# Sigmoid attention, last batch: unit 2 sorted earlier with a second set of rows, unit 3's root behind the last sigmoid

## The chip, the core and the metric

The kernel runs on one core of a Trainium2 chip. A core has five engines that run side by side and wait for each other by semaphores: TensorE (PE, matrix products), VectorE (DVE), ScalarE (ACT), GpSimd (POOL) and SyncE (SP, which only issues transfers). The metric is the device time of one execution in microseconds (us), lower is better.

## The reference

A block of four layers on x of 4 x 1024 tokens with 128 features: a sigmoid attention, an expert layer (8 experts, the best 2 of each token), a softmax attention, and the expert layer again. Only the end of the first and the start of the second matter here:

```python
q = jnp.einsum('bsd,ed->bse', x, Wq) + bq        # k and v alike
scores = jnp.einsum('bse,bte->bst', _layer_norm(q), _layer_norm(k)) / jnp.sqrt(jnp.float32(D))
attn = jax.nn.sigmoid(scores - jnp.log(jnp.float32(S)))
out = jnp.einsum('bst,bte->bse', attn, v)
x = x + (jnp.einsum('bsd,ed->bse', out, Wo) + bo) * layerscale
...
xf = _layernorm(x, ln_g, ln_b)                    # x normalised once before
logits = xf @ router_w
scores, idx = jax.lax.top_k(logits, 2)
gate = jax.nn.softmax(scores, axis=-1)
...                                               # each expert normalises xf again (z) and runs its MLP
```

## The kernel before

**Tiling.** Tokens lie 128 to a tile, 8 tiles to a batch (TPB = 8). Sigmoid attention takes the four batches in turn. A batch has 16 steps u. In each, TensorE computes a block of scores, ScalarE its sigmoid (line 389), and TensorE the product with v (line 295). TensorE holds one block of scores ahead. In the last batch (b = 3) the steps run over the first 512 queries (u = 0 to 7), then the second 512.

**Sorting beside it.** For the expert layer each token is written twice (once per chosen expert, k = 0 and 1) into a DRAM array, f_sorted, at a slot that groups the tokens by expert. This is done by unit: units 0, 1 and 2 are the batches 0, 1 and 2 with 8 tiles each, units 3 and 4 the two halves of batch 3 with 4 tiles each. A unit goes through these steps:

- VectorE: statistics of X (`tokens_to_sort`); ScalarE: `root` (the square root needs a load of its function table, and the next sigmoid needs another); VectorE: `invert(n, 0)`.
- Normal rows l_hat (ScalarE `scalar_rows` for units 0 to 2, VectorE `vector_rows` for 3 and 4); gain and shift make l_rows of them (GpSimd `pool_gain`, `pool_shift`, lines 891 and 896, for 0 to 2; VectorE `vector_gain`, lines 905 and 906, for 3 and 4).
- VectorE: statistics of l_rows (`sorted_rows`); ScalarE: second `root`; VectorE: `invert(n, 1)`; ScalarE `scalar_z` (line 1051) normalises l_rows in place.
- Beside that, the choice of the experts: TensorE `turn` transposes l_hat, ScalarE `copy_turned`, TensorE `route` (router product), VectorE `take_logits` and `pick`, TensorE `count`, VectorE `find_slots` (ends with the cast at line 1188).
- GpSimd writes the token numbers into the last column of the rows (iota, line 909) and issues one scatter per tile and copy (line 936). Units 0 to 2 have one set of rows, so the numbers of the second copy wait until the first eight scatters have landed. Units 3 and 4 have a second set (l_again), which ScalarE copies (`scalar_second_z`, line 1058).

What sets the order is the code: each engine runs a list written out by hand (`sort_in_last(u)` for ScalarE and for TensorE, `last_batch()` for VectorE, the block of GpSimd). Buffers of rows are shared: units 0 and 3, 1 and 4, and 2 alone. Arrays of statistics are shared by 0, 1, 2 and 4; unit 3 has its own. The expert layer begins when all engines have ended this block, GpSimd with a wait for all landings (`pool_end`).

Beside that, the weights of the experts are folded: GpSimd multiplies (line 688), TensorE makes bias terms (line 698), VectorE adds them (`fold_biases`, lines 709 to 711), SyncE stores them.

## Time and profile before

| | us |
|---|---|
| median of 3 runs | 2541.86 (2539.79 to 2549.73) |
| the profiled execution | 2537.98 |
| its span, first to last instruction | 2536.1 |
| TensorE busy | 2306.2 (91%) |
| VectorE busy | 2218.5 (87%) |
| ScalarE busy | 1652.6 (65%) |
| GpSimd busy | 1483.1 (58%) |

The sigmoid attention and the sorting take the first 270 us of the span, the expert layer up to some 500, softmax attention the most of the rest. The change touches only the stretch from 184 to 271 us. A row of a timeline tells start, duration, engine, line, operation, out<-in with shapes, how many are merged, and in square brackets how long the engine was idle ahead and what ended that. Buffer numbers are left out of names. The steps of GpSimd that issue a scatter show as DMA_INDIRECT; their duration is that of the issue, not of the transfer.

### The profile page before, as it was taken

The page shows a single profiled execution, that of the slowest core. Times are in us where ns is not written, and L with a number is a line of the kernel's source. Part 1 is how long each engine was busy: PE and PEld are TensorE (multiplying, and loading weights), DVE is VectorE, ACT ScalarE, POOL GpSimd, SP SyncE. Part 2 cuts the span into 40 slices and gives each one's busy share as a digit, 9 for nine tenths or more (in the row PEclk, how much of TensorE's full clock was granted, in tenths as well). Part 3 has the DMA queues.
Part 4 walks back from the last instruction along what each step waited for, and adds up shares of the span by engine and source line. Part 5 has one row for each costly group of instructions (what it writes and reads, how often), then busy time and mean ns, then how long its engine had stood idle before and what let it go on. Part 6 is the DMA issues. An engine that isn't in the chain of part 4 may idle for free. (4 is left out here: it accounts for less than half of the span.)

```text
span 2536.1 us, 44098 instructions
## 1 busy us (share of the span) xinstructions
PE 2306.2 (91%) x14954; PEld 1766.5 (70%) x14954; DVE 2218.5 (87%) x4734; ACT 1652.6 (65%) x2883; POOL 1483.1 (58%) x1075
## 2 busy tenths in 40 slices
PE   6996699658999999999999999999999999968995
PEld 3553588536777777777777777777777777747884
DVE  6766588779999999999999999999999999956886
ACT  2464244347777777787778778788778877743443
POOL 1145344326666666667668766676876766663442
PEclk8997799869999999999999999999999999988997
DMA  8821566654534454344322333223342233006665
GB/s 206 221 64 46 161 210 215 174 132 108 126 84 97 98 128 99 84 101 110 84 62 71 87 81 88 62 62 79 86 100 62 62 79 86 15 27 196 202 212 180
DMA packets 169648, 281.89 MB, mean 111 GB/s; under 512 B 32940, under 2 KB 122930, under 8 KB 169424
## 3 DMA queue, kind: packets, MB, share of 16 engines
q1 hardware_dynamic: 160208, 260.11, 40.6%
q0 software_dynamic: 9216, 18.96, 2.1%
q8 instruction: 120, 1.97, 0.3%
q14 instruction: 104, 0.85, 0.1%
HBM read 118.94 MB, written 62.39 MB: 72 GB/s over the span
## 5 line engine op out<-in xcount | busy, mean ns | idle before, releaser
L2438 POOL TENSOR_TENSOR b_prob<-b_prob,b_weight 128x1024 f32<-128x1024 f32 x512 | 958.7, 1905 | 505.5 <-DVE b_weight L2396 504.3
L2366 DVE TENSOR_REDUCE b_bmax<-b_score 128x16 f32<-128x1024 f32 x512 | 620.5, 1212 | 44.8 <-PE b_score L2217 29.3
L2318 ACT ACTIVATE b_prob<-b_score,b_neg_m 128x1024 f32<-128x1024 f32 x512 | 581.4, 1136 | 76.9 <-DVE b_neg_m L2374 75.1
L2353 DVE TENSOR_REDUCE b_bsum<-b_prob 128x16 f32<-128x1024 f32 x512 | 605.5, 1202 | 0.0
L2303 ACT ACTIVATE b_pT<-b_turn 128x512 f32<-128x512 f32 x1024 | 560.4, 609 | 63.4 <-PE b_turn L2230 55.2
L2230 PE MATMUL b_turn<-ident,b_prob 128*128 128x128 f32 x4096 | 532.1, 273 | 3.7 <-ACT b_pT L2303 3.6
L2230 PEld LDWEIGHTS b_turn<-ident,b_prob 128*128 128x128 f32 x4096 | 477.7, 140 | 75.7 <-ACT b_pT L2303 3.9
L2217 PE MATMUL b_score<-b_KH,b_QS 128*128 128x512 f32 x1024 | 478.8, 468 | 16.8 <-ACT b_prob L2318 14.6
L2197 PE MATMUL b_acc<-b_pT,b_V 128*64 128x256 f32 x4096 | 470.3, 382 | 0.0
L2217 PE MATMUL b_score<-b_KL,b_QS 128*128 128x512 f32 x1024 | 405.6, 396 | 0.0
L2197 PEld LDWEIGHTS b_acc<-b_pT,b_V 128*64 128x64 f32 x4096 | 282.7, 137 | 150.7 <-issue 21.4
L1719 ACT ACTIVATE f_e_act<-f_e_x,f_e_w 128x256 f32<-128x256 f32 (+1 forms) x320 | 155.0, 484 | 233.7 <-DVE f_e_x L1775 206.3
L2217 PEld LDWEIGHTS b_score<-b_KH,b_QS 128*128 128x128 f32 x1024 | 194.2, 190 | 142.9 <-issue 82.7
L1775 DVE TENSOR_SCALAR f_e_x<-f_e_p,f_e_w 128x256 f32<-128x256 f32 (+1 forms) x320 | 162.2, 507 | 76.7 <-PE f_e_p L1667 40.1
L2217 PEld LDWEIGHTS b_score<-b_KL,b_QS 128*128 128x128 f32 x1024 | 195.0, 190 | 41.5 <-issue 13.9
L1667 PE MATMUL f_e_p<-f_e_zT,f_e_w 128*128 128x256 f32 (+1 forms) x640 | 181.2, 365 | 3.8 <-ACT f_e_zT L1714 1.1
L2322 ACT ACTIVATE b_fall<-b_run_max 128x64 f32<-128x64 f32 x128 | 33.0, 258 | 224.2 <-DVE b_run_max L2380 209.0
L1668 PE MATMUL f_e_p<-f_e_zT,f_e_w 128*128 128x256 f32 (+1 forms) x640 | 176.7, 358 | 0.0
L1741 POOL TENSOR_SCALAR f_e_hT<-f_e_hid 128x512 f32<-128x512 f32 (+1 forms) x80 | 44.9, 561 | 220.0 <-DVE f_e_hid L1783 220.0
L1732 POOL DMA_INDIRECT f_outputs<-f_e_y,f_e_dest x142 | 143.2, 1008 | 36.3 <-issue 36.3
L1783 DVE SCALAR_TENSOR_TENSOR f_e_hid<-f_e_p,f_e_w,f_e_act 128x256 f32<-128x256 f32 (+1 forms) x320 | 142.4, 445 | 2.3 <-ACT f_e_act L1719 1.6
L2376 DVE TENSOR_TENSOR_SCAN b_run_max<-b_first_low,b_bmax 128x64 f32<-128x64 f32 x128 | 144.0, 1125 | 0.0
(329 smaller groups left out, 2956.6 us busy)
## 6 DMA issues: line engine op xcount, KB each, us to landing
f_e_w<-f_weights SPq DMA_DIRECT2D x80, 776.0 KB
f_sorted<-zeros SPq DMA_DIRECT2D x172, 193.5 KB, 5.4
b_KH<-b_k_high SPq DMA_DIRECT2D x128, 256.0 KB
b_KL<-b_k_low SPq DMA_DIRECT2D x128, 256.0 KB
b_QS<-b_q_high SPq DMA_DIRECT2D x64, 256.0 KB, 3.8
b_QS<-b_q_low SPq DMA_DIRECT2D x64, 256.0 KB, 4.9
b_hb<-b_hT SPq DMA_DIRECT2D x31, 512.0 KB
f_e_z<-f_sorted SPq DMA_DIRECT2D x62, 129.0 KB
```

Of the source, the lines that this page charges most:

```text
L1667: pe.matmul(p2[deep][:, 0:rows_of[t]], up_w(t, 1, c), zT[i][:, 0:rows_of[t]], start=True, stop=True).then_inc(x2_done, 1)
L1668: pe.matmul(p1[deep][:, 0:rows_of[t]], up_w(t, 0, c), zT[i][:, 0:rows_of[t]], start=True, stop=True).then_inc(up_done, 1)
L1719: act.activation(act2[c % 2][:, 0:rows_of[t]], x2[c % 2][:, 0:rows_of[t]], ACT.Silu, bias=bias(t, 1, c)).then_inc(act_ready, 1)
L1775: dve.tensor_scalar(x2[c % 2][:, 0:rows_of[t]], p2[(HC * i + c) % DEEP][:, 0:rows_of[t]], bias(t, 2, c), bias(t, 3, c), ALU.max, ALU.min). ...
L2197: last = pe.matmul(acc[h * HD:(h + 1) * HD, 0:QT * P], V[par][:, kt, h * HD:(h + 1) * HD], pT(g, kp)[h][:, kk * QT * P:(kk + 1) * QT * P], ...
L2217: last = pe.matmul(score[k % 2][:, c * HALF:(c + 1) * HALF], QS[par][h][:, q * P:(q + 1) * P], Kx[par][h][:, c * HALF:(c + 1) * HALF], sta ...
L2230: last = pe.transpose(turn[h][:, (kk * QT + q) * P:(kk * QT + q + 1) * P], prob[gr % 4][h * QT + q][:, (2 * k + kk) * P:(2 * k + kk + 1) * P],
L2303: act.activation(pT(g, k)[h][:], turn[h][:], ACT.Copy).then_inc(evac, 1)
L2318: act.activation(prob[r % 4][k][:], score[k % 2][:], ACT.Exp, bias=neg_m[r % 2][:, k:k + 1]).then_inc(prob_ready, 1)
L2353: dve.tensor_reduce(bsum[r % 2][:, k, :], prob[r % 4][k][:].rearrange("p (n c) -> p n c", c=KV_BLOCK), AX, ALU.add).then_inc(sum_ready, 1)
L2366: maxima = chain.mark(dve.tensor_reduce(bmax[r % 2][:, k, :], score[k % 2][:].rearrange("p (n c) -> p n c", c=KV_BLOCK), AX, ALU.max))
L2438: pool.tensor_tensor(tile, tile, weight[r % 2][:, k, :].unsqueeze(2).to_broadcast([P, NB, KV_BLOCK]), ALU.mult).then_inc(scaled, 1)
```

## The change

In the last batch:

- **VectorE** makes gain and shift of unit 2 (`vector_gain`, two passes over 128x1024), instead of GpSimd. `invert(2, 0)` stands ahead of the last `fold_biases`. Picking, inverting and finding the slots of unit 2 stand ahead of the update of X of batch 3's first half and of the statistics of unit 3. The slots of unit 3 stand ahead of the normal rows of unit 4.
- **TensorE**: unit 2's turns and routes at steps 6 to 8 instead of 7 to 10, its count at step 10 instead of 15.
- **ScalarE**: copies of the turned blocks at steps 6 and 7 (before 7 and 8), second root of unit 2 at 9 (before 13), its z rows at 11 and 12 (before 15 and behind the loop), then a copy of them into a second set of rows at 13 (new). The root of unit 3 stands behind the last sigmoid (step 15) instead of at 13.
- **GpSimd**: gain and shift of unit 2 go; unit 1's second copy no longer has them ahead of it; unit 2 is numbered in both sets at once and its 16 scatters follow each other without a wait for a landing.
- A new buffer again2 of 128 x 8 x 129 values. The second expert layer's sort keeps its way (BY_POOL and TWICE per layer).

```diff
                 fold.pool(pool, 6, 8)
-                sorter.pool_number(pool, 1, 0)
-                sorter.pool_scatter(pool, 1, 0, 0, TPB)
-                sorter.pool_gain(pool, 2)
-                sorter.pool_shift(pool, 2)
-                sorter.pool_number(pool, 1, 1)
-                sorter.pool_scatter(pool, 1, 1, 0, TPB)
                 for k in range(2):
-                    sorter.pool_number(pool, 2, k)
-                    sorter.pool_scatter(pool, 2, k, 0, TPB)
-                for n in (3, 4):
+                    sorter.pool_number(pool, 1, k)
+                    sorter.pool_scatter(pool, 1, k, 0, TPB)
+                for n in (2, 3, 4):
                     sorter.pool_number_both(pool, n)
-                for n in (3, 4):
+                for n in (2, 3, 4):
                     sorter.pool_scatter_both(pool, n)
...
                 def sort_in_last(u):
+                    if u == 6:
+                        sorter.turn(pe, 2, 0, ring[0])
                     if u == 7:
-                        sorter.turn(pe, 2, 0, ring[0])
-                    if u == 8:
                         sorter.route(pe, 2, 0, ring[0])
                         sorter.turn(pe, 2, 1, ring[1])
+                    if u == 8:
+                        sorter.route(pe, 2, 1, ring[1])
                     if u == 9:
                         project_back(BATCH - 1, 0)
                     if u == 10:
-                        sorter.route(pe, 2, 1, ring[1])
-                    if u == 15:
                         pe.wait_ge(sorter.logits_taken, sorter.halves(3))
                         sorter.count(pe, 2, ring[0])
...
-                    if u == 7:
-                        sorter.copy_turned(act, 2, 0, ring[0][:])
+                    if u in (6, 7):
+                        sorter.copy_turned(act, 2, u - 6, ring[u - 6][:])
                     if u == 8:
                         copy_out(BATCH - 1, 0)
-                        sorter.copy_turned(act, 2, 1, ring[1][:])
+                    if u == 9:
+                        sorter.root(act, 2, 1)
+                    if u in (11, 12):
+                        sorter.scalar_z(act, 2, u - 11)
                     if u == 13:
-                        sorter.root(act, 2, 1)
+                        sorter.scalar_second_z(act, 2)
+                    if u == 15:
                         sorter.root(act, 3, 0)
-                    if u == 15:
-                        sorter.scalar_z(act, 2, 0)
...
-                sorter.scalar_z(act, 2, 1)
                 sorter.copy_turned(act, 3, 0, ring[1][:])
...
                     update(BATCH - 2)
                     tokens_to_sort(2)
+                    invert(2, 0)
                     fold_biases(BATCH - 1)
-                    invert(2, 0)
+                    sorter.vector_gain(dve, chain, 2)
                     sorted_rows(2)
-                    update_half(BATCH - 1, 0)
-                    tokens_to_sort(3)
                     for half in range(2):
                         sorter.take_logits(dve, 2, half, ring[half])
                     sorter.pick(dve, chain, 2)
                     invert(2, 1)
+                    sorter.find_slots(dve, chain, 2, ring[0])
+                    update_half(BATCH - 1, 0)
+                    tokens_to_sort(3)
                     invert(3, 0)
                     sorter.vector_rows(dve, 3)
-                    sorter.find_slots(dve, chain, 2, ring[0])
                     sorter.vector_gain(dve, chain, 3)
...
                     invert(4, 0)
+                    sorter.find_slots(dve, chain, 3, ring[1])
                     sorter.vector_rows(dve, 4)
-                    sorter.find_slots(dve, chain, 3, ring[1])
                     sorter.vector_gain(dve, chain, 4)
```

Where it shows in the program, engine by engine. GpSimd, from the end of unit 1's gain on, before (l0_rows0 to l0_rows2 are the three sets of rows, l0_slots0 to 2 their slots):

```order
L909 IOTA l0_rows1 128x8
L936 DMA f_sorted0<-l0_rows1,l0_slots1 33024x129 x8
L891 TENSOR_TENSOR l0_rows2<-l0_hat0,l0_gain 128x8x128
L896 TENSOR_TENSOR l0_rows2<-l0_rows2,l0_shift 128x8x128
L909 IOTA l0_rows1 128x8
L936 DMA f_sorted0<-l0_rows1,l0_slots1 33024x129 x8
L909 IOTA l0_rows2 128x8
L936 DMA f_sorted0<-l0_rows2,l0_slots2 33024x129 x8
L909 IOTA l0_rows2 128x8
L936 DMA f_sorted0<-l0_rows2,l0_slots2 33024x129 x8
```

and now:

```order
L911 IOTA l0_rows1 128x8
L938 DMA f_sorted0<-l0_rows1,l0_slots1 33024x129 x8
L911 IOTA l0_rows1 128x8
L938 DMA f_sorted0<-l0_rows1,l0_slots1 33024x129 x8
L911 IOTA l0_rows2 128x8
L911 IOTA l0_again2 128x8
...
L938 DMA f_sorted0<-l0_rows2,l0_slots2 33024x129 x8
L938 DMA f_sorted0<-l0_again2,l0_slots2 33024x129 x8
```

The two passes of gain and shift are gone, all numbering stands ahead of unit 2's scatters, and no numbering stands between its two copies.

ScalarE, from the copy-out of the first half to that of the second (a_AT are the sigmoids, l_0_std unit 2's root, l_1_std unit 3's), before:

```order
L360 ACTIVATE a_oT<-a_acc 128x512
L994 ACTIVATE l_0_xfT<-a_ring,l_columns 128x512
L389 ACTIVATE a_AT<-a_score,a_neg_log 128x512 x5
L1002 ACT_TABLE_LOAD
L1002 ACTIVATE l_0_std<-l_0_var 128x8
L1002 ACTIVATE l_1_std<-l_1_var 128x4
L389 ACT_TABLE_LOAD
L389 ACTIVATE a_AT<-a_score,a_neg_log 128x512 x2
L1051 ACTIVATE l_rows<-l_rows,l_0_bias,l_0_rstd 128x128 x4
L360 ACTIVATE a_oT<-a_acc 128x512
```

and now, from the root of unit 2 on:

```order
L1004 ACTIVATE l_0_std<-l_0_var 128x8
L385 ACT_TABLE_LOAD
L385 ACTIVATE a_AT<-a_score,a_neg_log 128x512 x2
L1054 ACTIVATE l_rows<-l_rows,l_0_bias,l_0_rstd 128x128 x4
L385 ACTIVATE a_AT<-a_score,a_neg_log 128x512
L1054 ACTIVATE l_rows<-l_rows,l_0_bias,l_0_rstd 128x128 x4
L385 ACTIVATE a_AT<-a_score,a_neg_log 128x512
L1061 ACTIVATE l_again<-l_rows 128x8x128
L385 ACTIVATE a_AT<-a_score,a_neg_log 128x512 x2
L1004 ACT_TABLE_LOAD
L1004 ACTIVATE l_1_std<-l_1_var 128x4
L354 ACTIVATE a_oT<-a_acc 128x512
```

Both passes over unit 2's rows and the copy stand between sigmoids, and the root of unit 3 behind the last of them.

VectorE, after the inversion for unit 4 (l_0_bias), before:

```order
L1038 TENSOR_SCALAR l_hat<-X,l_0_rstd,l_0_bias 128x128 x4
L1159 MEMSET l_1_per_tile 128x8x4
...
L1188 CAST l_slots<-l_1_slot_f 128x2x4
L905 TENSOR_TENSOR l_rows<-l_hat,l_gain 128x4x128
L906 TENSOR_TENSOR l_rows<-l_rows,l_shift 128x4x128
```

and now:

```order
L1162 MEMSET l_1_per_tile 128x8x4
...
L1191 CAST l_slots<-l_1_slot_f 128x2x4
L1041 TENSOR_SCALAR l_hat<-X,l_0_rstd,l_0_bias 128x128 x4
L907 TENSOR_TENSOR l_rows<-l_hat,l_gain 128x4x128
L908 TENSOR_TENSOR l_rows<-l_rows,l_shift 128x4x128
```

Unit 3's slots (l_1) are found ahead of unit 4's normal rows (l_hat), which TensorE turns.

## Rows read from the trace of the kernel before

**Rows 1.** Busy by stage: from:to, us; PE, PEld, DVE, ACT, POOL busy; clock; DMA; GB/s.

```profile
192.00:196.00 4.00, 4.00 (x6) 1.65 (x6) 0.00 (x0) 0.06 (x1) 1.95 (x3) 0.57 0.71 246
...
208.00:220.00 12.00, 11.58 (x39) 5.78 (x37) 8.49 (x44) 6.71 (x11) 7.07 (x7) 1.00 0.14 44
...
237.00:249.00 12.00, 4.00 (x16) 3.43 (x16) 10.67 (x56) 4.06 (x9) 8.69 (x14) 0.50 0.14 45
249.00:271.00 22.00, 0.00 (x0) 0.00 (x0) 4.28 (x19) 1.03 (x2) 15.51 (x18) 0.50 0.15 48
```

**Rows 2.** GpSimd's timeline: start, duration, line, operation, idle before and what ended it.

```profile
193.60 0.96 POOL L936 DMA_INDIRECT f_sorted<-l_rows,l_slots  x1 [0.30 <-issue]
201.59 2.35 POOL L891 TENSOR_TENSOR l_rows<-l_hat,l_gain 128x1024 f32<-128x1024 f32 x1 [7.04 <-ACT l_hat L1027]
...
225.21 0.14 POOL L909 IOTA l_rows<- 128x8 f32 x1 [8.32 <-ACT l_rows L1051]
...
237.28 0.15 POOL L909 IOTA l_rows<- 128x8 f32 x1 [1.41 <-DMA f_sorted<-l_rows,l_slots]
...
240.27 1.34 POOL L936 DMA_INDIRECT f_sorted<-l_rows,l_slots  x1 [0.30 <-issue]
...
248.99 0.98 POOL L936 DMA_INDIRECT f_sorted<-l_rows,l_slots  x1 [0.53 <-issue]
...
267.96 0.96 POOL L936 DMA_INDIRECT f_sorted<-l_again,l_slots  x1 [0.30 <-issue]
270.84 0.15 POOL L1284 IOTA f_e_small_number<- 128x9 f32 x1 [1.92 <-POOLq L128]
```

**Rows 3.** ScalarE's timeline, the last batch.

```profile
197.68 1.65 ACT L1027 ACTIVATE l_hat<-X,l_bias,l_rstd 128x128 f32<-128x128 f32 x4 [0.88 <-DVE l_bias L1103]
...
214.46 0.69 ACT L389 ACTIVATE a_AT<-a_score,a_neg_log 128x512 f32<-128x512 f32 x1 [1.92 <-PE a_acc L295]
216.18 0.69 ACT L389 ACTIVATE a_AT<-a_score,a_neg_log 128x512 f32<-128x512 f32 x1 [1.03 <-PE a_acc L295]
...
218.50 1.28 ACT L389 ACT_TABLE_LOAD   x1
219.80 1.26 ACT L389 ACTIVATE a_AT<-a_score,a_neg_log 128x512 f32<-128x512 f32 x2
...
223.50 1.64 ACT L1051 ACTIVATE l_rows<-l_rows,l_bias,l_rstd 128x128 f32<-128x128 f32 x4
...
236.69 0.63 ACT L1058 ACTIVATE l_again<-l_rows 128x512 f32<-128x512 f32 x1
```

**Rows 4.** VectorE's timeline, units 2, 3 and 4.

```profile
206.23 1.65 DVE L1070 BATCH_NORM_STATS2 l_parts<-l_rows 128x6 f32<-128x128 f32 x8 [8.59 <-POOL l_rows L896]
...
224.36 0.17 DVE L1188 CAST l_slots<-l_slot_f 128x16 uint32<-128x16 f32 x1
224.47 0.69 DVE L905 TENSOR_TENSOR l_rows<-l_hat,l_gain 128x512 f32<-128x512 f32 x1
...
227.32 0.68 DVE L463 TENSOR_TENSOR a_upd<-a_proj,a_bo 128x512 f32<-128x512 f32 x1
...
236.28 1.11 DVE L1038 TENSOR_SCALAR l_hat<-X,l_rstd,l_bias 128x128 f32<-128x128 f32 x4
...
239.25 0.17 DVE L1188 CAST l_slots<-l_slot_f 128x8 uint32<-128x8 f32 x1
...
242.21 0.18 DVE L1108 COPY l_logits<-a_ring 128x32 f32<-128x32 f32 x1
...
248.29 0.19 DVE L1188 CAST l_slots<-l_slot_f 128x8 uint32<-128x8 f32 x1
```

**Rows 5.** TensorE's timeline: turn and route of unit 4.

```profile
237.53 1.09 PE L963 MATMUL a_ring<-ident,l_hat 128*128 128x128 f32 x4 [2.60 <-DVE l_hat L1038]
239.49 1.88 PE L973 MATMUL a_ring<-l_rw,l_xfT 128*128 128x8 f32 x8 [0.87 <-ACT l_xfT L994]
```

More of the change, by code:

```diff
@@ L780 @@
 WHOLE = 3
+BY_POOL = (2, 3)
+TWICE = ((2, 3, 4), (3, 4))
 BUFFERS = ((0, 1, 2, 0, 1), (0, 0, 0, 1, 0))
@@ L823, in pooled, with copies @@
     def pooled(self, n):
-        return WHOLE * self.layer + n
+        return sum(BY_POOL[0:self.layer]) + n
+    def copies(self, n):
+        return sum(len(u) for u in TWICE[0:self.layer]) + TWICE[self.layer].index(n)
     def moved_once(self, n):
@@ L933, in pool_scatter @@
     def pool_scatter(self, pool, n, k, first, end):
-        rows = self.second_rows[n] if k and n >= WHOLE else self.rows[n]
+        rows = self.second_rows[n] if k and n in TWICE[self.layer] else self.rows[n]
         for i in range(first, end):
@@ L1014, in hat_free @@
             eng.wait_ge(self.turned, self.halves(users[-1] + 1))
-            eng.wait_ge(self.scaled, self.pooled(users[-1]) + 1)
+            if users[-1] < BY_POOL[self.layer]:
+                eng.wait_ge(self.scaled, self.pooled(users[-1]) + 1)
     def scalar_rows(self, act, n, half):
@@ L1063, in statistics @@
         if which and half == 0:
-            if n < WHOLE:
+            if n < BY_POOL[self.layer]:
                 dve.wait_ge(self.xf_ready, self.pooled(n) + 1)
@@ L2483, in program @@
             hats = [mine(f"hat{i}", [P, TPB, D])[:] for i in range(2)]
-            again = [mine(f"again{i}", [P, TPB // 2, WITH_ID])[:] for i in range(2)]
+            again = [mine("again2", [P, TPB, WITH_ID])[:]] + [mine(f"again{i}", [P, TPB // 2, WITH_ID])[:] for i in range(3, 5)]
             short = slice(0, TPB // 2)
             arrays = [SortArrays(mine, f"{i}_") for i in range(2)]
-            sorter.begin(mine, 0, folded.sorted_rows[0], rows + [rows[0][:, short, :], rows[1][:, short, :]], [None] * WHOLE + again,
+            sorter.begin(mine, 0, folded.sorted_rows[0], rows + [rows[0][:, short, :], rows[1][:, short, :]], [None] * 2 + again,
                          [hats[0]] * WHOLE + [hats[1][:, short, :], hats[0][:, short, :]], places + places[0:2],
```

2 lines of the change are left out of this document (1 added, 1 removed).

## The prediction

> **What bounds the kernel now.** I read the busy time by stage first, then the four engines' timelines of the last batch. The table by stage [rows 1] shows what the change can reach: between 249 and 271 us TensorE does nothing, VectorE is busy 4.28 of 22 us, and GpSimd 15.51. The stretch is GpSimd alone: it issues the scatters that put rows in expert order, and the expert layer can't start before the last one has landed. In GpSimd's own timeline [rows 2] the scatters of units 3 and 4 run from 248.99 to 267.96 without a wait, 15 steps in 18.97 us, so 1.265 us a scatter; the last is issued at 268.92 and GpSimd's first instruction of the next stage starts at 270.84, 1.92 us later.
>
> How late GpSimd starts on them is the question, and unit 2 answers it. GpSimd sat idle 8.32 us before 225.21 waiting for ScalarE's normalised rows of unit 2 (l_rows), issued eight scatters from 225.6, waited 1.41 us for their landing because the same buffer needs other row numbers for the second copy, and issued eight more up to 248. From there it never catches up. Meanwhile unit 3's slots are known at 239.25 + 0.17 = 239.42 and unit 4's at 248.29 + 0.19 = 248.48 [rows 4]: unit 3's eight scatters could have gone out ten us before they did. So the end has two constraints: GpSimd's backlog, which ends it now, and behind it VectorE's last slots, 248.48.
>
> **The change, part by part.**
>
> *Unit 2's rows sooner.* VectorE now does gain and shift of unit 2 itself. Before, it sat idle 8.59 us up to 206.23 for GpSimd's two passes, which began at 201.59 [rows 2, 4]: 4.64 us. VectorE's pass over 512 columns takes 0.69 us [rows 4]; twice the columns cost between 1.2 (only the columns double, and some 0.2 us is fixed) and 1.38 us each, so 2.5 us for two; gain 2.1. Unit 2's inversion also moves ahead of the bias folding: ScalarE waited 0.88 us for it before 197.68 [rows 3], gain 0.85. Statistics of the sorted rows so begin at about 203.2 instead of 206.23.
>
> *The two routings and the root.* Turn and route are each one or two loop steps sooner, the root of unit 2 goes from step 13 to step 9, and its two table loads (1.28 us each) go with it: moved, not removed. With the roots they held the next sigmoid from 216.87 to 219.80, 2.93 us [rows 3]. With the routing done near 206.9, picks, inversion and count in the order the code gives, I get the bias of unit 2 at 211.4 and its slots at 214.1 against 224.36 + 0.17 = 224.53 [rows 4]. The normalised rows are made in steps 11 and 12, 1.64 us each [rows 3], and end near 215.7 instead of 223.50 + 1.64 = 225.14. Bounds: the loop's step 13 began at 216.18 [rows 3]; if nothing of the loads (2.93) and of the two row passes (3.3) now ahead of it is hidden, unit 2's rows are ready at 222.4, still 2.7 sooner. I take 215.7, because the loop is paced by TensorE there, ScalarE having waited 1.03 us before 216.18, and similar waits before the steps ahead of it take the work in.
>
> *The second set of rows.* Sixteen scatters of unit 2 go out back to back. Added: one copy on ScalarE of 1024 columns, about twice the 0.63 us of 512 columns [rows 3], so 1.1 to 1.3, in step 13; it is needed only 10.1 us after the first scatter. Removed: the wait of 1.41 us. GpSimd queue: unit 1's second eight scatters move ahead, from 206 to some 196 to 206.5 (the first eight ended at 193.60 + 0.96, plus 1.4 for landing). Behind them stands the numbering of units 2, 3 and 4, all with buffers free by 208. SyncE is passed by nothing but a bias store about 1.6 us later, with nobody behind it in this stretch. GpSimd: 215.9 + 16 x 1.265 = 236.1; with 0.3 for a stretched scatter, a little less than the one at 240.27 [rows 2], 236.4.
>
> *Unit 3.* Its root now stands behind the last sigmoid. Before, the last two sigmoids ran at 219.80 to 221.06, held up by two table loads [rows 3]. With the loads at step 9 and the two passes and the copy (4.4 us) ahead of the last sigmoid I work out 218.6 for its start, so the root ends at 218.6 + 0.6 + 1.28 + 0.2 = 220.7. This is an added wait for VectorE: it has done update and statistics of unit 3 by 217.7 and stands idle 3 us, with its whole tail queued behind: inversion 1.2, unit 3's rows 1.1, gain and shift 1.45, statistics 1.4. Then the last update begins at 226.05, where it began at 227.32 [rows 4]: 1.27 sooner. From there the sequence is the old one, except that unit 3's slots now go ahead of unit 4's rows: the rows, from 236.28, took 1.08 us of VectorE's time ahead of them [rows 4]; now 239.42 - 1.27 - 1.08 = 237.07. Bounds for the last sigmoid's end: 221.06 - 2.93 = 218.1 (the loads go, all else hides), and 221.06 + 4.4 = 225.5 (nothing hides), against my 219.2.
>
> *Unit 4.* This is where the 1.27 goes. Its rows now end after unit 3's slots, at 239.36 - 1.27 = 238.1. From rows to routed logits the path goes through TensorE at the low clock (0.50) [rows 1]: turn began at 237.53, route at 239.49 and lasted 1.88 [rows 5], that is 4.0 from the rows' end to its end, or 242.2. VectorE, with only gain and statistics (2.85 us) between, would be there at 241.0: it waits 1.2 us and takes the logits at 242.2, as before at 242.21 [rows 4]. Slots of unit 4: 248.5, unchanged.
>
> *Sum.* Unit 3's eight scatters: from 237.25, the slots, not the backlog of 236.4; 10.1 us plus 0.4 for one stretched as at 240.27 [rows 2], ready at 247.8. Unit 4: from the slots, 248.65 with the same small gap; the last issue ends at 248.65 + 8 x 1.265 - 0.3 = 258.5 against 268.92. Gain 10.4 us. VectorE's block table, which follows its last slots and is the 4.28 us busy after 249 [rows 1], ends near 254 and stays hidden. The profiled execution took 2537.98 (span 2536.1), which gives 2527.6 (span 2525.7). That execution was 3.9 below the median of the runs shown; against the median, 2541.86, the same gain gives 2531.4, which I take.
>
> GpSimd and VectorE meet in the tail. A scatter takes 0.96 us, but 1.34 at 240.27, while VectorE is in gain and shift of unit 4 [rows 2]: 0.4 for the pair of passes, counted above. The Trainium skill, in "SBUF — State Buffer", section "SBUF: two separate sides", makes the shared port an exclusive lock, held for the whole instruction by a VectorE operation with two SBUF inputs against a GpSimd operation that reads SBUF. The trace agrees in direction, with 0.4 us of the 1.4 that the pair lasts.
>
> **Rivals.**
> 1. *The lock in full.* Six such passes (gain and shift of unit 3, two of the update, gain and shift of unit 4) lie beside scatters now, at 0.69 us each 4.1 instead of 0.7. Unit 2's would end at 238.6, unit 3's at 250.4, the last issue at 260.2: gain 8.7, 2533.2. Against it: only 0.4 of 1.4 at 240.27. It is what the Trainium skill's rule of the same section says if the scatter waits out each pass in full.
> 2. *More: the sigmoid loop runs ahead.* If the stall around 192 to 196, at a granted clock of 0.57 [rows 1], is shorter in the new order, or route(4) is faster, units 3 and 4 come up to 1.6 us sooner: gain 12.0, 2529.9. GpSimd's backlog forbids more: 215.9 + 32 x 1.265 + 0.7 - 0.3 = 256.8, gain 12.1 even with all slots at hand, unless unit 2 is itself sooner.
> 3. *The work doesn't hide in the loop.* By the bounds: root of unit 3 ends 6.3 later than I take it, slots of unit 4 at 248.5 + 6.3 = 254.8, gain 4.1, 2537.8. For it: ScalarE carries 7.3 us of inserted work between step 9 and the last sigmoid. Against it: the waits of ScalarE in the old loop.
> 4. *Slower: TensorE falls to the low clock in the loop.* TensorE waits for held-up sigmoids; at 192 to 196 the clock was 0.57 after a stretch of one-column matmuls [rows 1]. A score and a product together pace the sigmoids at 1.72 us (214.46 to 216.18 [rows 3]); at the low clock they take twice that. From step 9 on some 6.5 such pairs are left, 11.2 us more, plus the 6.3 of rival 3 on top: it decides from a delay of the last sigmoid by 10.4 us. Both together give 17.5 later, 7.1 slower: 2549.0. Against it: the waits of 1 us in the loop of before left the clock at 1.00 from 208 to 220 [rows 1].
>
> **How the numbers follow.** Forecast (gain 9.4 to 11.4) 0.60; the lock 0.08; ahead 0.14; not hidden 0.13; slower 0.05. A measurement of this kernel can tell about 0.5%, 12.7 us, from no change, so the forecast itself lies within it. Faster by more than that needs rival 2 and the scatter of the runs (2539.79 to 2549.73): half of 0.14 and a tenth of 0.60, 0.13. Slower 0.05, within 0.82. The range goes from rival 2 against the fastest run shown (2539.79 - 12.1 = 2527.7), less the 1.8 by which the profiled one lies below it and 2 of spread, to rival 3 with 2 of spread: 2524 to 2540.
>
> **What would show it.** Right: sixteen unbroken scatters from near 216, no wait for a landing; unit 3's from 237.3; a short idle of GpSimd, under 1 us, before unit 4's at 248.7; VectorE idle some 3 us before inverting unit 3 and some 1.2 before unit 4's logits; next stage at 260.4. Wrong: the first scatter of unit 2 after 218 (work not hidden), the last sigmoid after 220, scatters of 1.6 us (lock), a clock of 0.5 before 220, or unit 4's slots away from 248.5; then the gain follows unit 4's slots one for one.

## The result, and the profile after

The changed kernel took 2538.0 us (median of 20 runs), the kernel before 2542.07 in the same rounds: a ratio of 0.9984 [0.9977, 0.9992], so 4.1 us gained (2.0 to 5.8) where 10.4 was forecast. Its profiled execution took 2539.82 us (span 2537.8).

The busy time by stage, as in [rows 1]:

```profile
192.00:196.00 4.00, 4.00 (x19) 2.61 (x20) 1.36 (x9) 1.83 (x3) 3.09 (x4) 0.73 0.21 59
208.00:220.00 12.00, 10.72 (x37) 6.24 (x37) 6.62 (x30) 9.56 (x16) 2.15 (x8) 0.86 0.03 11
237.00:249.00 12.00, 1.85 (x8) 1.64 (x8) 6.25 (x33) 2.27 (x5) 5.32 (x6) 0.50 0.09 28
249.00:271.00 22.00, 3.18 (x14) 2.71 (x12) 12.31 (x61) 4.77 (x9) 14.95 (x18) 0.50 0.15 49
```

Between 237 and 249 us no engine is now busy for much more than half of the time, where VectorE was busy 10.67 of 12 before, and after 249 VectorE still has 12.31 us to do. GpSimd's timeline, against [rows 2]:

```profile
221.69 0.98 POOL L938 DMA_INDIRECT f_sorted<-l_rows,l_slots  x1 [10.05 <-ACT l_rows L1054]
...
229.31 1.45 POOL L938 DMA_INDIRECT f_sorted<-l_rows,l_slots  x1 [0.30 <-issue]
231.06 0.96 POOL L938 DMA_INDIRECT f_sorted<-l_rows,l_slots  x1 [0.30 <-issue]
232.33 1.27 POOL L938 DMA_INDIRECT f_sorted<-l_again,l_slots  x1 [0.30 <-issue]
...
241.49 0.96 POOL L938 DMA_INDIRECT f_sorted<-l_again,l_slots  x1 [0.30 <-issue]
247.79 1.08 POOL L938 DMA_INDIRECT f_sorted<-l_rows,l_slots  x1 [5.33 <-DVE l_slots L1191]
...
259.06 0.96 POOL L938 DMA_INDIRECT f_sorted<-l_rows,l_slots  x1 [1.07 <-issue]
...
270.66 0.15 POOL L1287 IOTA f_e_small_number<- 128x9 f32 x1 [1.78 <-issue]
```

Sixteen unbroken scatters of unit 2 and no wait for a landing, as meant; but then GpSimd waits 5.33 us for unit 3's slots, which the forecast had ready 0.85 us behind its backlog. VectorE's timeline, against [rows 4], tells why:

```profile
211.50 0.19 DVE L1111 COPY l_logits<-a_ring 128x32 f32<-128x32 f32 x1 [3.84 <-PE a_ring L975]
...
226.09 0.18 DVE L1097 RECIPROCAL l_rstd<-l_std 128x4 f32<-128x4 f32 x1 [3.14 <-ACT l_std L1004]
...
231.36 0.68 DVE L458 TENSOR_TENSOR a_upd<-a_proj,a_bo 128x512 f32<-128x512 f32 x1
...
237.84 0.17 DVE L1097 RECIPROCAL l_rstd<-l_std 128x4 f32<-128x4 f32 x1
238.94 0.22 DVE L1098 TENSOR_TENSOR l_square<-l_rstd 128x4 f32<-128x4 f32 x1 [0.93 <-DVE l_rstd L1097]
239.19 0.16 DVE L1099 TENSOR_TENSOR l_fix<-l_square,l_var 128x4 f32<-128x4 f32 x1
240.35 0.17 DVE L1104 TENSOR_SCALAR l_square<-l_fix 128x4 f32<-128x4 f32 x1 [1.00 <-DVE l_fix L1099]
241.05 0.17 DVE L1105 TENSOR_TENSOR l_rstd<-l_rstd,l_square 128x4 f32<-128x4 f32 x1 [0.53 <-DVE l_square L1104]
...
243.18 0.16 DVE L1098 TENSOR_TENSOR l_square<-l_rstd 128x4 f32<-128x4 f32 x1 [1.67 <-remote]
...
246.83 0.17 DVE L1191 CAST l_slots<-l_slot_f 128x8 uint32<-128x8 f32 x1
...
252.05 0.19 DVE L1111 COPY l_logits<-a_ring 128x32 f32<-128x32 f32 x1 [0.98 <-PE a_ring L975]
...
258.11 0.17 DVE L1191 CAST l_slots<-l_slot_f 128x8 uint32<-128x8 f32 x1
```

From 237.84 to 245.0 VectorE does the two inversions, 12 instructions that start 0.2 us apart in other traces (2.5 us for all), and takes 7 us for them: six of them start 0.4 to 1.7 us behind the end of the one before. Five of these waits are for the instruction before on the same engine, the one of 1.67 has no releaser on this core (`remote`). I call such a stretch a hole: an engine stands idle although nothing that the profile shows on this core holds it. Unit 4's turn and route stand 10.65 us later than in [rows 5], and take as long as before:

```profile
248.18 1.09 PE L965 MATMUL a_ring<-ident,l_hat 128*128 128x128 f32 x4 [9.08 <-DVE l_hat L1041]
250.14 1.88 PE L975 MATMUL a_ring<-l_rw,l_xfT 128*128 128x8 f32 x8 [0.87 <-ACT l_xfT L996]
```

ScalarE's timeline, against [rows 3], has a second hole, a wait of 3.77 us that the profile puts down to nothing on this core:

```profile
208.51 0.78 ACT L996 ACTIVATE l_xfT<-a_ring,l_columns 128x512 f32<-128x512 f32 x1 [3.77 <-remote]
...
219.29 1.64 ACT L1054 ACTIVATE l_rows<-l_rows,l_bias,l_rstd 128x128 f32<-128x128 f32 x4
...
221.40 1.05 ACT L1061 ACTIVATE l_again<-l_rows 128x1024 f32<-128x1024 f32 x1
...
223.85 0.69 ACT L385 ACTIVATE a_AT<-a_score,a_neg_log 128x512 f32<-128x512 f32 x1 [0.83 <-PE a_score L210]
```

Behind that wait the granted clock fell to 0.50 from 211 to 214 us, where it had been 1.00 before. The batch's first sigmoid starts at 185.88 us, 1.81 later than before, ahead of all that was changed. So from here on times are counted from that sigmoid (184.07 in the trace before), and "next stage" is the first IOTA row behind the last scatter. The expectations below, from the second group on, count the next stage from the sequencer's record 0.4 us ahead of that row (76.2 there is 76.6 here).

### The profile page after: what moved, and what is told of

Its sections match the earlier page's. It is cut to its first block and busy times, and to the rows that moved or that the text cites. A ratio compares the mean times of both kernels' runs of the same rounds, so it can differ in the third digit from the quotient of the medians.

```text
span 2537.8 us, 44100 instructions
## 1 busy us (share of the span) xinstructions
PE 2309.0 (91%) x14954; PEld 1768.7 (70%) x14954; DVE 2223.1 (88%) x4736; ACT 1652.7 (65%) x2884; POOL 1479.4 (58%) x1073
## 5 line engine op out<-in xcount | busy, mean ns | idle before, releaser
L2321 ACT ACTIVATE b_prob<-b_score,b_neg_m 128x1024 f32<-128x1024 f32 x512 | 581.8, 1136 | 76.2 <-DVE b_neg_m L2377 73.3
L2306 ACT ACTIVATE b_pT<-b_turn 128x512 f32<-128x512 f32 x1024 | 560.7, 609 | 62.8 <-PE b_turn L2233 57.1
```

Source lines behind the costliest of these rows:

```text
L2306: act.activation(pT(g, k)[h][:], turn[h][:], ACT.Copy).then_inc(evac, 1)
L2321: act.activation(prob[r % 4][k][:], score[k % 2][:], ACT.Exp, bias=neg_m[r % 2][:, k:k + 1]).then_inc(prob_ready, 1)
```

## The experiments

The chip changed between groups of runs, and that turned out to matter. Where the kernel before took 2541 to 2543 us (the result, the second and the fifth group), all eight traces, of whatever kernel, have holes such as the two above; I call these chips A. Where it took 2531.5 to 2532.4 (the other three groups), twelve traces have none of them; chips B. So A and B are told apart by the time and the holes together. The table holds what the reading rests on, in us after the first sigmoid:

| | unit 2's first scatter | last sigmoid ends | root of unit 3 | slots 3 | slots 4 | next stage |
|---|---|---|---|---|---|---|
| forecast of after | 31.8 | 35.1 | 36.6 | 53.0 | 64.4 | 76.3 |
| after, the result's trace (A) | 35.8 | 38.7 | 40.2 | 61.1 | 72.4 | 84.8 |
| after, fourth trace (A) | 32.6 | 35.4 | 36.9 | 57.3 | 68.6 | 81.0 |
| after, second and third (B) | 32.1 | 35.0 | 36.5 | 52.9 | 64.1 | 76.5 |
| before (A) | 41.6 | 37.0 | 34.4 | 55.4 | 64.4 | 86.8 |
| before, second and third (B) | 40.0 | 35.4 | 32.8 | 53.8 | 62.8 | 85.2 |

**The same kernels again (B).** The two kernels unchanged.

> The changed kernel once more, for a second profile. In its first profile unit 4's slots came at 258.28, 10 us later than forecast, through three holes: ScalarE 3.77 us before the second turned copy of unit 2, TensorE at the low clock from 210 to 214, and VectorE stretched by 5.0 us in the inversions at 238 to 245. Theory A (the holes are chance of one execution, late arrivals of semaphores): this profile doesn't show the 5.0 at the same instructions, unit 4's slots come 67.5 to 69 us after the batch's first sigmoid instead of 72.4, the next stage starts 78 to 80 us after it instead of 84.8, and the time ratio is near 0.996. Theory B (the holes belong to the order of instructions, e.g. where an engine's code is fetched): the same instructions stall again, 72.4 and 84.8 within 0.5, ratio 0.998.

> The kernel before once more, for a second profile. If GpSimd's backlog set its end, the last scatter follows the first scatter of unit 2 by 43.3 us again whatever VectorE's slots do, and the next stage starts 86.8 us after the batch's first sigmoid, within 1. Theory A (holes by chance): the wait of 5.30 us of VectorE before the last bias folding and where ScalarE waits on nothing that the profile shows change by over 1 us. Theory B: they stand again where they were, within 0.5.

The ratio is 0.9967 [0.9955, 0.9978], 8.4 us. The holes are gone and with them 8.2 us of the stage; both kernels' next stage came sooner than I had expected (76.2 and 84.8 as counted there, for 78 to 80 and 86.8). VectorE and GpSimd, of the changed kernel's second trace:

```profile
211.30 0.19 DVE L1097 RECIPROCAL l_rstd<-l_std 128x8 f32<-128x8 f32 x1
211.53 0.17 DVE L1098 TENSOR_TENSOR l_square<-l_rstd 128x8 f32<-128x8 f32 x1
211.73 0.17 DVE L1099 TENSOR_TENSOR l_fix<-l_square,l_var 128x8 f32<-128x8 f32 x1
```

```profile
217.68 0.98 POOL L938 DMA_INDIRECT f_sorted<-l_rows,l_slots  x1 [6.61 <-ACT l_rows L1054]
...
239.18 0.98 POOL L938 DMA_INDIRECT f_sorted<-l_rows,l_slots  x1 [0.75 <-DVE l_slots L1191]
...
250.41 0.96 POOL L938 DMA_INDIRECT f_sorted<-l_rows,l_slots  x1 [1.14 <-DVE l_slots L1191]
...
262.09 0.15 POOL L1287 IOTA f_e_small_number<- 128x9 f32 x1 [1.88 <-POOLq L128]
```

The linked steps are 0.2 us apart, and GpSimd's waits ahead of units 3 and 4 are 0.75 and 1.14. So the holes don't belong to the kernel alone. Chance of one execution (theory A) isn't shown by it, since the chip was another one: on chips A holes came in every later trace too. The kernel before is 1.6 us shorter as well, all of it ahead of unit 2's first scatter: from that scatter on both its traces take 45.2 us.

**One part of the change at a time (B).** Unit 4's rows ahead of unit 3's slots again:

```
-                    sorter.find_slots(dve, chain, 3, ring[1])
                     sorter.vector_rows(dve, 4)
+                    sorter.find_slots(dve, chain, 3, ring[1])
```

> The changed kernel with unit 4's rows ahead of unit 3's slots on VectorE again, as before. If unit 4's slots set the end and the path from its rows through TensorE holds VectorE: unit 4's logits are taken without a wait, its slots come 1.0 us sooner after the last sigmoid's root than in the changed kernel, unit 3's slots 1.1 later, GpSimd's wait ahead of unit 3 grows by 1.1 and the one ahead of unit 4 vanishes: then GpSimd's run of unit 3 sets the end and the stage ends within 0.3 of the changed kernel. If GpSimd's backlog doesn't matter at all and only slots 4 do: 1.0 us sooner.

Ratio 0.9963 [0.9952, 0.9975]. The loop took 1.7 us longer in this trace, although the program up to there is that of the changed kernel. TensorE was longer at the low clock. These are the stages from 5 to 16 us after the first sigmoid, of the changed kernel's second trace and of this one (the clock is the number ahead of the last two):

```profile
190.54:201.54 11.00, 11.00 (x42) 6.30 (x43) 2.17 (x13) 7.95 (x15) 6.10 (x8) 0.84 0.34 111
```

```profile
187.25:198.25 11.00, 11.00 (x39) 6.71 (x39) 1.91 (x12) 6.31 (x12) 5.99 (x8) 0.69 0.34 111
```

So I count from the root of unit 3: slots 4 come 1.14 us sooner than in the changed kernel (26.4 for 27.6), GpSimd waits 1.81 for unit 3 and nothing for unit 4, and the next stage starts 0.5 later. That part of the change is worth half a microsecond in the trace; the times can't tell it from nothing.

The second set of rows alone, in the old order:

```
-                for n in (3, 4):
+                for n in (2, 3, 4):
                     sorter.pool_scatter_both(pool, n)
...
                 sorter.scalar_z(act, 2, 1)
+                sorter.scalar_second_z(act, 2)
```

> The kernel before with the second set of rows for unit 2 alone (one copy more on ScalarE behind the last sigmoid, GpSimd's and VectorE's order otherwise as before). Theory 1 (GpSimd's backlog sets the end of before): unit 2's scatters start at the same place, run 16 in a row, and the last scatter ends 2.6 to 2.9 us sooner relative to the first scatter of unit 2 (40.5 instead of 43.3); stage 84.0 us from the first sigmoid instead of 86.8; ratio 0.999. Theory 2 (the end is set elsewhere, by slots 4): no gain, and the copy of 1.1 us on ScalarE delays unit 3's roots: 0 to 1.1 us slower.

Ratio 0.9982 [0.9974, 0.9991], so 4.6 us in the time (2.3 to 6.6); last scatter 2.7 us sooner, next stage at 82.6 instead of 85.2: 2.6 in the trace, as theory 1 has it. GpSimd's backlog sets the end of the kernel before, and the order brings the rest of the 8.7.

**Is the chain through unit 4's slots the bound?** Fourteen short linked statistics ahead of unit 4's picks, in both kernels:

```
                     sorter.take_logits(dve, 4, 0, ring[0])
+                    for again in range(14):
+                        chain.link(dve.bn_stats(sorter.arrays[4].parts[:, 0, :], X[:, UNITS[4][0], :]))
                     sorter.pick(dve, chain, 4)
```

> The changed kernel with 14 short linked statistics put ahead of unit 4's picks on VectorE, 3.4 us of added time in unit 4's chain. Theory (in the changed kernel unit 4's slots set the end, so each delay of that chain counts in full): slots of unit 4, GpSimd's start on them and the next stage are all 3.4 us later relative to unit 3's root than in the undisturbed profile of the changed kernel (slots 27.58 to 31.0 us after it, next stage 39.65 to 43.0), GpSimd's wait ahead of unit 4 grows from 1.14 to 4.5, and the ratio to the kernel before is 0.9967 + 0.0013 = 0.998. Rival (GpSimd's own 32 scatters in a row are the bound): under 1 us later, ratio 0.9967.

> The same 14 statistics in the kernel before. Theory (GpSimd's backlog sets its end and hides what comes late in VectorE's chain): slots of unit 4 come 3.4 us later, at 66.3 us after the batch's first sigmoid instead of 62.8, GpSimd starts unit 4 at 73.4 as before without a wait, the next stage starts at 84.8, ratio 1.000. Rival (the slots matter there too): 3.4 us slower, ratio 1.0013.

This group ran on a chip A. The ratios are 0.9999 [0.9990, 1.0009] and 0.9993 [0.9983, 1.0004]: the changed kernel loses its whole gain, the kernel before nothing. But the trace of the first has a hole in the same stretch (the second root of unit 3 to slots 4 took 30.5 us), so here are both once more, on a chip B:

> The changed kernel with the 14 linked statistics (3.4 us) ahead of unit 4's picks, again, since the first time a stall of 3 to 5 us lay in the same stretch. Theory (unit 4's slots set the end, one for one): on a chip without stalls slots 4 at 64.1 + 3.4 = 67.5 us after the first sigmoid, next stage at 76.1 + 3.4 = 79.5, ratio 0.9967 + 0.0013 = 0.998. Rival (GpSimd's 32 scatters are the bound): next stage at most 1 later, 77.1.

> The same statistics in the kernel before, again. Theory (hidden under GpSimd's backlog): slots 4 at 66.3 instead of 62.8 us after the first sigmoid, next stage at 84.8, ratio 1.000. Rival: next stage 88.2, ratio 1.0013.

The statistics cost 4.4 us, 1.0 more than I had put. Slots 4 moved by 4.4 in both. The next stage moved by 4.4 in the changed kernel (76.5 to 80.9) and by -0.1 in the kernel before (85.2 to 85.1); ratios 0.9990 [0.9979, 1.0001] and 0.9995 [0.9985, 1.0004]. GpSimd's row for the start of unit 4, first of the changed kernel with the statistics, then of the kernel before with them:

```profile
253.05 0.95 POOL L940 DMA_INDIRECT f_sorted<-l_rows,l_slots  x1 [5.62 <-DVE l_slots L1193]
```

```profile
259.72 0.96 POOL L938 DMA_INDIRECT f_sorted<-l_rows,l_slots  x1 [0.30 <-issue]
```

The first waits 5.62 us for the slots, the second no longer than between any two scatters. So a delay of VectorE's chain counts in full in the changed kernel, and 4.4 us of it cost nothing in the old one, where unit 4's slots (248.48) lie 10.6 us ahead of their first scatter (259.12). That is what makes the holes matter to one and not to the other.

**Without the second set of rows, new order (A).**

```
-                for n in (2, 3, 4):
-                    sorter.pool_scatter_both(pool, n)
+                for k in range(2):
+                    sorter.pool_number(pool, 2, k)
+                    sorter.pool_scatter(pool, 2, k, 0, TPB)
```

> The changed kernel without the second set of rows for unit 2: GpSimd waits again for its first eight scatters to land. Theory (the backlog is just hidden in the changed kernel): unit 2's scatters end at 54.5 to 56.3 us after the first sigmoid instead of 52.9, beyond unit 3's slots at 52.9, so unit 3 starts 1 to 2.6 later than its 53.6, and the next stage starts 0.3 to 1.6 later than 76.2, less than the 2.6 that the set gave in the old order; ratio 0.997 to 0.9973. Rival (the set is what brings the gain in the new order too): 2.6 or more later, ratio 0.998.

The wait for the landing is back (1.49 us), unit 2's scatters end at 55.6, and unit 3's start at 56.7, behind its slots at 54.5. A hole of 2.7 us lies in unit 4's places, so its end says nothing. With the slots of the traces on chips B (52.9, 64.1), unit 3 would start at 54.9 and end at 65.0, 0.4 behind its place in the changed kernel: an estimate by which the second set, worth 2.6 in the old order, is worth 0.4 in the new one. The ratio, 0.9969 [0.9957, 0.9981], is no worse than the changed kernel's on other chips A (0.9984 and 0.9981). That speaks against 2.6, as far as holes cost as much on this chip as on those, which no run here shows.

**Unit 2's rows still sooner (A, then B).** ScalarE's rows, the turns, the routes and the second root one step ahead:

```
-                    if u in (4, 5):
-                        sorter.scalar_rows(act, 2, u - 4)
+                    if u in (3, 4):
+                        sorter.scalar_rows(act, 2, u - 3)
```

> The changed kernel with ScalarE's rows of unit 2 one sigmoid sooner, right behind the root and behind the next sigmoid, and turn, route and second root one step sooner too. ScalarE stood idle 2.65 us there and VectorE 6.88 us for those rows. Theory (unit 2's chain and ScalarE's load both count): VectorE's gain of unit 2 starts 2.4 us sooner after the first sigmoid (15.5 gets 13.1), the last sigmoid ends about 1.6 sooner (35.0 gets 33.4), next stage 74.5 instead of 76.2, ratio 0.996. Rival (TensorE's pace sets the loop there): the rows are sooner, the last sigmoid within 0.5, and the next stage within 0.5 of 76.2, ratio 0.9967.

> The kernel with unit 2's rows one sigmoid sooner, again. Its first profile had a stall of 4.5 us in the loop. Theory (its gain is 1.6 us where no stall falls in): on a chip without stalls the last sigmoid ends 33.4 us after the first one's start and the next stage starts at 74.5, ratio 0.996; on a chip with stalls the ratio is 0.0006 below that of the changed kernel in the same session. Rival (TensorE's pace sets the loop): last sigmoid at 35.0, next stage at 76.2.

A miss. Gain of unit 2 starts 1.2 us sooner on chip B, but the last sigmoid ends at 37.7 instead of 35.0 and the next stage starts at 79.1: ScalarE now waits 1.47 us for TensorE's turned rows ahead of sigmoid 6, where it had made sigmoid 6 first. This is not all the edit's doing: from 5 to 16 us after the first sigmoid the clock was 0.69, as in the trace of the version with unit 4's rows first, where it came with 1.7 us more loop and no edit ahead of it.

```profile
188.02:199.02 11.00, 11.00 (x38) 6.53 (x39) 3.41 (x14) 7.49 (x14) 6.21 (x8) 0.69 0.34 111
```

Less those 1.7, about 1.0 of the 2.7 is left to the edit: an estimate, and from one trace. The ratio, 0.9967 [0.9954, 0.9979], shows neither gain nor loss against the changed kernel, nor does the one on chip A, 0.9979 [0.9967, 0.9991], whose trace had a hole of 4.5 us in the loop. What is shown is that no gain came; that an earlier request to TensorE only stands in front of a sigmoid is my reading of the 1.47 us, not tested.

**Chips and the place in the program (B).**

> The changed kernel a third time. So far two chips were seen: on one (before at 2542 to 2543) every trace has stalls of 3 to 5 us that nothing in the profile explains, on the other (before at 2532) none of the four traces has one. Theory (the gain is 10 us less what of the stalls falls into the chain that now sets the end): on a chip without stalls the ratio is 0.9967 again, the next stage 76.2 us after the first sigmoid within 0.5, and unit 4's slots 22.0 us after the second root of unit 3; on a chip with them the ratio is 0.998 to 0.9985, and slots 4 are 25 to 27 us after that root. Rival (the difference of the two ratios is chance): ratio near 0.9976 on either.

> The kernel before a third time. Theory: the next stage starts 84.8 us after the batch's first sigmoid on a chip without stalls and 86.4 on one with them, since only a stall ahead of unit 2's first scatter moves its end; from that scatter to the next stage it is 44.8 us within 0.2 on both. Rival: that distance changes by over 1 us with a stall on VectorE.

> The changed kernel with 40 tiny memsets in VectorE's program behind the bias folding of the last batch, where VectorE stands idle 4.6 to 6.9 us, so that its later instructions lie 40 places further on. In four traces of the changed order on the chip with stalls, VectorE's linked small instructions went at 0.71 us instead of 0.20 around its instruction 702 to 717 (once 769 to 774), next to the fetch of an 8 KB piece of its program. Theory F (the stall goes with the place in the program): the fetch comes 40 instructions of work sooner, among unit 3's picks or before, and the stall with it; slots 4 still late by 3 to 5 us. Rival T (it goes with the work or the time): the stall stays at the inversions of units 3 and 4. On a chip without stalls neither shows: the memsets cost 0 to 0.5 us and the rest stands as it was.

> The changed kernel with 40 memsets in VectorE's program, again; the first time it ran on a chip without stalls, where the fetch moved from 233.7 to 219.5 us and no time changed. On a chip with stalls, theory F (the stall goes with the place in the program): VectorE's slow stretch lies next to the fetch, ahead of unit 3's picks. Rival T (with the work or the time): it stays at the inversions of units 3 and 4, 50 to 58 us after the first sigmoid. On a chip without stalls: next stage at 76.1 again, ratio 0.9967, and the question stays open.

The changed kernel: 0.9967 [0.9955, 0.9979] and every milestone within 0.1 us of the second trace, on another chip. The kernel before again takes 45.2 us from unit 2's first scatter to the next stage, and so it does with the statistics on a chip A (45.3). The 40 memsets cost nothing (0.9967 [0.9955, 0.9979] and 0.9964 [0.9951, 0.9978], next stage at 76.5 and 76.4). Both times the chip had no holes, so theory F and rival T were not told apart.

**Unit 3's root ahead of the last sigmoid (B).**

```
-                    if u == 15:
+                    if u == 14:
                         sorter.root(act, 3, 0)
```

> The changed kernel with unit 3's first root one step ahead of the last sigmoid instead of behind it: one table load more (1.28 us) ahead of the last sigmoid. Theory (VectorE's idle of 3.15 us for that root is at the head of the chain that sets the end, and the last sigmoid has slack): root 1.5 sooner, 35.0 instead of 36.5 us after the first sigmoid, last sigmoid 2.0 later, slots 4 at 62.6 to 63.0, next stage at 74.9 to 75.3, ratio 0.9963. Rival (the last sigmoid, through the update of the last half, holds the chain): last update 1 later than 41.8, next stage at 76.5 to 77.5, ratio 0.997.

Root at 35.0, last sigmoid 37.0, slots 4 at 63.2, next stage at 75.6, 1.0 sooner than the changed kernel; ratio 0.9959 [0.9946, 0.9973]. The steps on ScalarE:

```profile
217.17 0.68 ACT L385 ACTIVATE a_AT<-a_score,a_neg_log 128x512 f32<-128x512 f32 x1
217.87 1.28 ACT L1004 ACT_TABLE_LOAD   x1
219.16 0.20 ACT L1004 ACTIVATE l_std<-l_var 128x4 f32<-128x4 f32 x1
219.38 1.28 ACT L385 ACT_TABLE_LOAD   x1
220.68 0.69 ACT L385 ACTIVATE a_AT<-a_score,a_neg_log 128x512 f32<-128x512 f32 x1
```

Two loads of 1.28 and the root take 2.8 us, of which the last sigmoid had waited 0.83 anyway, so it is 2.0 later. The Trainium skill, in "ScalarE: Activation LUTs", section "What ACT_TABLE_LOAD costs", adds a drain of about 1.38 us to each load; here a load starts 0.02 us behind the instruction ahead of it, and the next one 0.01 to 0.02 us behind the load, so the measurement says otherwise. This is the best of the versions in the trace; in the time it can't be told from the changed kernel. The root behind the last sigmoid is a part of the change that costs, 1.0 us by this trace: VectorE's wait for it is 3.14 us at the head of the chain that sets the end, and 1.62 so.

**Both orders together, and the changed kernel a fourth time (A).**

> The changed kernel with unit 3's first root one step ahead of the last sigmoid and unit 4's rows ahead of unit 3's slots. In the version with the root alone GpSimd starts unit 3 right behind unit 2 (53.04 us after the first sigmoid) and waits 0.75 for unit 4's slots. Theory (this takes unit 4's slots under GpSimd's backlog, which then sets the end): slots 3 at 52.6, slots 4 at 62.2, GpSimd without a wait from the first scatter of unit 2 to the last, next stage at 74.6 to 74.9, ratio 0.9958. Rival: as the version with the root alone, 75.2, since unit 3 now waits for its slots. On a chip with stalls both are later by what falls into VectorE's chain.

> The changed kernel a fourth time. Theory: next stage at 76.1 and ratio 0.9967 on a chip without stalls; on one with stalls slots 4 are 25 to 27 us after the second root of unit 3 instead of 22.0, and the ratio is 0.998 to 0.9985. Rival: ratio 0.9984 on a chip without stalls too.

The changed kernel: 0.9981 [0.9969, 0.9993], on a chip A other than that of the second group. Up to the root of unit 3 its trace lies within 0.8 us of the forecast; then the inversions again, in VectorE's timeline:

```profile
233.44 0.18 DVE L1097 RECIPROCAL l_rstd<-l_std 128x4 f32<-128x4 f32 x1
234.57 0.16 DVE L1098 TENSOR_TENSOR l_square<-l_rstd 128x4 f32<-128x4 f32 x1 [0.96 <-DVE l_rstd L1097]
235.28 0.16 DVE L1099 TENSOR_TENSOR l_fix<-l_square,l_var 128x4 f32<-128x4 f32 x1 [0.54 <-DVE l_square L1098]
236.00 0.17 DVE L1104 TENSOR_SCALAR l_square<-l_fix 128x4 f32<-128x4 f32 x1 [0.56 <-DVE l_fix L1099]
237.41 0.16 DVE L1105 TENSOR_TENSOR l_rstd<-l_rstd,l_square 128x4 f32<-128x4 f32 x1 [1.23 <-DVE l_square L1104]
```

Slots 4 come 26.1 us after unit 3's second root, 22.0 on chips B: 4.1 late, and the stage 4.5. The version with both orders has its holes ahead of slots 3 (GpSimd waits 6.29 us for them) and gives 0.9987 [0.9976, 0.9998]: whether GpSimd's backlog is its bound stays open.

## Why the prediction was wrong

The range held the measured 2538.0, but the gain was 4.1 us, not 10.4, and by a path that no rival describes. Part by part:

**The bound.** Right. Before, GpSimd's backlog set the end (4.4 us more on VectorE moved it by -0.1); after, unit 4's slots do (4.4 moved it by 4.4).

**Unit 2's rows, routing, the second set.** Right where no hole fell in. VectorE's two passes take 1.23 each (I put 1.25); statistics of the sorted rows start at 19.2 and 19.1 on chips A (forecast 19.1) and at 18.0 on chips B, where a wait for the routed logits takes the difference up; slots of unit 2 at 29.8 on chips B (30.0), the first scatter at 32.1 (31.8). The copy takes 1.05. In the result's own trace, behind the hole of 3.77 us, the slots came at 33.5 and the first scatter at 35.8.

**Unit 3 and the root.** Right on chips B: the root ends at 36.5 (36.6), VectorE is idle 3.14 us for it (3), the update starts at 41.8 (42.0). In the result's trace they are at 40.2 and 45.5.

**Unit 4 through TensorE.** Right: a wait of 0.98 (1.2), slots 4 at 64.1 on chips B (64.4), next stage at 76.5 (76.3).

**The lock.** Rival 1 didn't come. Two scatters of unit 2 were stretched, 1.45 and 1.27 instead of 0.96, and one of unit 3, 1.21: 1.05 us in all, not the 4.1 that the lock in full asks for, and the same three are stretched in the traces on chips B. The Trainium skill's rule of "SBUF — State Buffer", section "SBUF: two separate sides", if a scatter waits out every pass, disagrees with that number.

**Rivals 3 and 4.** The time measured is that of rival 3 (2537.8), by coincidence. In the result's trace two of its signs came, the first scatter after 218 (221.69) and the last sigmoid after 220 (224.54), but behind a hole of 3.77 us and not from work that didn't hide: with the same program the last sigmoid ended at 35.4 in the fourth trace and at 35.0 on chips B (forecast 35.1). Rival 4's low clock came there too, 0.50 from 211 to 214 us, behind the same hole; in the second and the fourth trace the clock of 208 to 220 us was 1.00. It came as a consequence of a hole and cost a part of the 3.6 us by which the loop was late, not the 11.2 of rival 4.

**The step that failed.** It is "Slots of unit 4: 248.5, unchanged", the term from which the sum goes ("Unit 4: from the slots"). Counted from the first sigmoid they came at 72.4 and 68.6 on chips A, not at 64.4. I took VectorE's chain at the durations of its rows and put the holes at nothing, in a sum where for the first time each microsecond of that chain counts. The trace that I worked from had holes: a wait for nothing known of 5.30 us at 196.09, and linked steps 0.7 us apart at 156 to 158. These are VectorE's rows of the kernel before:

```profile
156.40 0.18 DVE L749 TENSOR_TENSOR a_qk_norm_square<-a_qk_norm_rstd 128x16 f32<-128x16 f32 x1 [0.38 <-DVE a_qk_norm_rstd L748]
157.11 0.17 DVE L750 TENSOR_TENSOR a_qk_norm_fix<-a_qk_norm_square,a_qk_norm_var 128x16 f32<-128x16 f32 x1 [0.54 <-DVE a_qk_norm_square L749]
...
196.09 0.17 DVE L709 TENSOR_TENSOR a_bout<-a_proj,a_b 128x8 f32<-128x8 f32 x1 [5.30 <-remote]
```

I read the stretch around the wait of 5.30 only as something that could get shorter (rival 2), and never asked what a hole of 4 us would do in the new chain, where 10 us of backlog no longer cover it. The two kinds of chip fall short of 10.4 by different terms. On chips A, where the result was timed, the stage of before is the 86.8 that I subtracted from. There the holes in VectorE's chain between unit 3's second root and slots 4 take 4.1 and 4.6 (fourth and first trace), and in the first trace the sigmoid loop was 3.7 longer, behind the hole of 3.77 us: stages of 81.0 and 84.8 against 86.8, so 5.8 and 2.0 gained, around the 4.1 and 4.8 timed there (the 4.8 from the ratio; the medians of that group differ by 3.1). On chips B, without holes, the gain is 8.7 us in the trace and 8.4 in the time: the stage of before is 85.2 there, since the 86.8 held 1.6 us of a hole ahead of its first scatter, and my stage after, 76.3, held none.

This account stops at the next stage, and on chips A the rest of the program is no constant either. ScalarE's last eight copies of b_oT, some 1900 us further on and not touched by the change, take 77.2 us from the first start to the last in all twelve traces on chips B. On chips A they take 81.8 and 85.1 in the two traces of the old order and 84.1 to 84.9 in the six of the new one. This is the wait in the result's trace:

```profile
2249.84 0.38 ACT L2300 ACTIVATE b_oT<-b_acc 128x256 f32<-128x256 f32 x1 [8.04 <-remote]
```

So the pair of profiled executions of the result differs by 3.1 us there, against the changed kernel; whether that is chance or follows from the change, two traces of the old order can't tell, and part of the missing gain on chips A may lie there.

**What stays open.** What the holes are, and whether their place is chance. VectorE's slow stretch between its instructions 702 and 717 (once 769 to 774) of those in the trace is there in all six traces of the new order on chips A, and in neither of the two of the old order there. Two traces are few. A piece of an engine's program is fetched next to it in five of the six, but also at the same instructions in the traces without a hole:

```profile
q14 instruction: 1, 0.01, 0.5%
```

That is the DMA table of the second trace of the changed kernel between 230 and 240 us, where nothing stalls. The Trainium skill, in "Runtime: NRT & Kernel Launch", section "Instruction fetch mechanics", has this fetch mostly hidden; the fetch alone costs nothing measurable here either. The runs with 40 memsets, meant to tell, came on chips without holes. The slow steps between 155 and 164 us on chips A begin 0.2 to 2.0 us behind a fetch of 16 KB in all eight traces; the same fetch stands at the same work in eight of the twelve traces on chips B, with no slow step.

## What to carry to other kernels

A queue that is behind (here GpSimd, by 10 us) covers late signals for as long as it is behind: 4.4 us of them cost nothing here. A change that takes the backlog away makes a chain of dozens of short linked instructions the bound, and such a chain is as long as its undisturbed rows only on an undisturbed chip: price a gain of this kind once more with the holes that the trace of before shows anywhere moved into the new chain, and subtract stages that are either both with or both without them.

Ask of each part what it is worth in the new order, not in the old one: the second set of rows gave 2.6 us alone, and by an estimate 0.4 beside the new order.

## What the runs showed of the hardware

Chips differ. The same kernel takes 2541 to 2543 us on some and 2531.5 to 2532.4 on others, and what the traces show of the difference is a few holes at the same places of the program. On three chips without them twelve traces have no linked step of VectorE more than 0.3 us behind the one it waits for. On the chips with them all eight traces have such steps or shorter ones (0.15 us behind and more) between 155 and 164 us, three to five of them in seven and one in the eighth, with starts 0.7 us apart where 0.2 is the rule; a wait of 2.5 to 5.3 us without a releaser on this core ahead of VectorE's last bias folding; and 4.6 to 7.9 us more in ScalarE's last eight copies of b_oT, 7.2 on average, which is the most of the 10 us. How the chips differ otherwise, and why, no run here shows. Without holes, the milestones of the changed kernel repeat within 0.1 us over four traces on three chips, two of them with the memsets (the next stage within 0.15).

A chip without holes still has a loop of two lengths: with TensorE's clock at 0.84 over the stretch from 5 to 16 us after the first sigmoid the root of unit 3 ends at 36.5, with 0.69 there 1.7 us later, with the same program up to that root. A table load took 1.28 us and no more when the next instruction is on the same engine.
